# The value projection beside query and key, and V placed by DMA through DRAM

## The chip, the cores and the metric

The kernel runs on one core of a Trainium2 chip. The metric is the device time of one execution in microseconds (us); smaller is better. One execution was also taken by the hardware profiler, and its trace is what is read here.

## What is computed

Eight batches of 256 tokens with 128 features go through one transformer layer. Attention has 16 heads of 8 dimensions, and a token sees only tokens at most 32 away. A mixture of 8 experts follows.

```
h    = layernorm(x) * (1 + ca) + sa
qkv  = h @ W_qkv.T                      # Q, K, V: 16 heads of 8
attn = softmax(Q K^T / sqrt(8) within 32 tokens)
x    = x + ga * (attn V) @ W_o.T
h    = layernorm(x) * (1 + cb) + sb
x    = x + gb * experts(h)              # top 2 of 8, silu(g) * u @ down
```

## The kernel before

One engine program is written by hand for each engine, and semaphores tie them together. The work is a software pipeline over the eight batches. In step `i` every engine does the attention of batch `i`, the part after attention (output projection, second norm, routing) of batch `i - 1`, the experts of batch `i - 2`, and the query and key projection of batch `i + 1`. The order inside a step is the order of the calls in each engine's `step`, and an engine executes its program strictly in that order. TensorE is PE, VectorE is DVE, ScalarE is ACT, GpSimd is POOL, SyncE is SP.

A batch is cut in 8 key blocks of 32 tokens (`NKB`, `KB`). The 16 heads are 4 groups (`NHG`) of 4 (`G`), and in `v_bd` the four heads `g` of a group have 32 partitions each. The names that matter below:

- `h_t` (128 features x 256 tokens) is written by ACT in `modulate_x` (L387). `project_qk` (L531 key, L532 query) and `project_v` (L539) read it on PE. In `step` on PE `project_v(i)` stands after `scores(i, 0)` and `transpose_o(i - 1)`, and `project_qk(i + 1)` stands after `down`.
- `keep_k` (DVE, L805) and `keep_q` (ACT, L393) copy the projections from PSUM (the bank groups `W2` and `W0`) to `k_bd` and `q_sb`, which `scores` needs.
- `keep_v` (ACT, L402) copies V from PSUM bank `OB` into `v_bd`, the block-diagonal operand that holds, for each key block and group of heads, 32 columns of V and 4 columns that sum the denominator. Each of its 16 copies takes 32 partitions x 64 elements. It stands between the exponentials of half 0 and `tanh_gate(i - 2, 1)`.
- `weigh_values` (PE, L583) multiplies `v_bd` with the probabilities. Its first call in a step, for half `t = 0`, waits for `v_ready` of that batch.
- `scores(i, t)` (L552, and L559 for the mask) is followed by `block_max` (DVE, L813), `row_maximum` (L831), `subtract_max` (PE, L567) and `exponentials` (ACT, L435). `activate` (DVE, L905 and L909) gates the experts, `weigh_experts` (POOL, L323) scales them, `transpose_act` (PE, L636) and `down` (L643) finish them.
- `route_input` (ACT, L417) hands the logits (PE, L594) to the routing chain on DVE, which ends in `cw` (L897).
- SP's queue carries the loads of `x` (L266) and the stores of `out` (L270). A store waits for `out_ready`.

## Time and profile before

| | before |
|---|---|
| median of 3 runs | 197.63 us (197.5 to 197.66) |
| the profiled execution's own time | 195.44 us |
| its span in the trace | 193.7 us |
| PE busy | 151.8 us, 78% |
| DVE busy | 141.0 us, 73% |
| ACT busy | 99.9 us, 52% |
| POOL busy | 49.6 us, 26% |

The span is the time between the first and the last instruction in the trace; the execution's own time holds 1.7 us more around it. Busy shares are means over stages with different limits, so no engine that is at 78% need be the limit at a given moment. The trace lists instructions in order of time. An engine's idle time stands in square brackets with the engine, tile and line that ended it.

### The profile page before, as it was taken

What the parts mean: (1) busy time and instruction counts of PE and PEld (TensorE: products, weight loads), DVE (VectorE), ACT (ScalarE), POOL (GpSimd) and SP (SyncE); (2) the same over time, 40 slices, a digit from 0 to 9 for tenths busy, and PEclk for the clock granted to TensorE, in tenths of its full rate; (3) what the DMA queues carried; (4) which work ended last, traced back from release to release, by engine and by line L of the source; (5) the groups of instructions that cost most, each with busy time, mean ns of one, the idle gap of its engine ahead of it and who ended that gap; (6) DMA issues with size and microseconds to landing.
All of it is one profiled execution on the core that took longest, in us unless ns stands there. A gap on an engine that the chain in (4) does not pass through costs nothing.

```text
span 193.7 us, 5025 instructions
## 1 busy us (share of the span) xinstructions
PE 151.8 (78%) x1948; PEld 126.1 (65%) x1948; DVE 141.0 (73%) x381; ACT 99.9 (52%) x262; POOL 49.6 (26%) x79
## 2 busy tenths in 40 slices
PE   1653986869995998699877987799779976975944
PEld 1553966658774885588656866596558765954744
DVE  2477166466779798788969796979697959856762
ACT  3170543945385538663667457654944494543420
POOL 5070000112052123232233205320530143224130
PEclk9995899975999999999999999999999999999987
DMA  5910000100000020001000010000000000000001
GB/s 141 279 41 0 3 3 0 30 3 0 3 0 0 3 54 3 0 5 36 21 3 3 8 50 0 2 3 27 3 0 3 27 5 0 5 27 0 0 0 54
DMA packets 5831, 4.12 MB, mean 21 GB/s; under 512 B 816, under 2 KB 5424, under 8 KB 5808
## 3 DMA queue, kind: packets, MB, share of 16 engines
q1 hardware_dynamic: 5664, 3.80, 6.9%
q8 instruction: 15, 0.25, 0.5%
q14 instruction: 8, 0.07, 0.1%
q10 hardware_dynamic: 144, 0.00, 0.0%
HBM read 2.76 MB, written 1.05 MB: 20 GB/s over the span
## 4 chain that ended last, share of the span: by engine, by line
PE 48%; DVE 23%; issue 19%; POOL 4%; ACT 4%; DMA 1%; DVEq 0%; POOLq 0%; ACTq 0%
PE ps L552 9%; DVE blkmax L813 8%; PE ps L643 7%; PE ps L583 7%; PE ps L567 4%; DVE gate_a L905 3%; POOL act_w L323 3%; PE ps L621 3%; DVE act L909 3%; DVE xn L790 3%; PE ps L636 3%; PE ps L623 2%; PE ps L622 2%; PE ps L594 2%; PE ps L531 2%
## 5 line engine op out<-in xcount | busy, mean ns | idle before, releaser
L813 DVE TRANSPOSE_TENSOR_REDUCE blkmax<-ps 128x44 f32<-128x1408 f32 x16 | 26.4, 1647 | 17.1 <-PE ps L559 17.1
L323 POOL TENSOR_TENSOR act_w<-act,cw 128x512 f32<-128x512 f32 x15 | 15.6, 1043 | 67.8 <-issue 48.7
L583 PE MATMUL ps<-probs,v_bd 128*36 128x64 f32 (+2 forms) x640 | 23.6, 229 | 8.4 <-ACT v_bd L402 8.4
L583 PEld LDWEIGHTS ps<-probs,v_bd 128*36 128x36 f32 x640 | 21.6, 115 | 12.8 <-issue 12.3
L402 ACT ACTIVATE v_bd<-ps 32x64 f32<-32x64 f32 x128 | 27.4, 214 | 1.8 <-PE ps L539 0.4
L435 ACT ACTIVATE probs<-ps 128x704 f32<-128x704 f32 x32 | 23.0, 756 | 5.2 <-PE ps L567 5.0
L552 PEld LDWEIGHTS ps<-q_sb,k_bd 32*128 32x128 f32 x640 | 19.3, 186 | 3.4 <-issue 2.4
L552 PE MATMUL ps<-q_sb,k_bd 32*128 32x96 f32 (+2 forms) x640 | 21.3, 274 | 0.1
L636 PE MATMUL ps<-con,act_w 128*128 128x128 f32 x64 | 10.3, 283 | 11.4 <-POOL act_w L323 5.7
L448 ACT ACTIVATE tanh_g<-ps 128x512 f32<-128x512 f32 x16 | 9.6, 597 | 17.6 <-PE ps L623 16.6
L567 PE MATMUL ps<-shift,quad_ones 128*128 128x384 f32 x64 | 16.7, 386 | 1.6 <-DVE shift L831 0.8
L643 PE MATMUL ps<-wd_sb,act_t 128*128 128x128 f32 x128 | 17.4, 293 | 0.7 <-ACT act_t L452 0.7
L643 PEld LDWEIGHTS ps<-wd_sb,act_t 128*128 128x128 f32 x128 | 16.5, 207 | 1.0 <-ACT act_t L452 0.9
L636 PEld LDWEIGHTS ps<-con,act_w 128*128 128x128 f32 x64 | 6.8, 142 | 14.7 <-POOL act_w L323 7.5
L805 DVE TENSOR_TENSOR k_bd<-ps,con 128x1024 f32<-128x1024 f32 x8 | 9.8, 1226 | 8.1 <-DVE ebeat L853 4.7
L452 ACT ACTIVATE act_t<-ps 128x512 f32<-128x512 f32 x16 | 9.6, 598 | 11.6 <-PE ps L636 11.6
L831 DVE TENSOR_TENSOR shift<-row_max,con 128x256 fp32r<-128x256 f32 x32 | 15.1, 513 | 0.6
L621 PE MATMUL ps<-w_hi,h_hi 128*128 128x512 f32 x32 | 14.0, 437 | 1.6 <-DVE act L909 1.4
L442 ACT ACTIVATE o_t<-ps 36x512 f32<-36x512 f32 x16 | 9.5, 592 | 9.3 <-PE ps L583 9.1
L567 PEld LDWEIGHTS ps<-shift,quad_ones 128*128 128x128 f32 x64 | 11.0, 206 | 4.0 <-DVE shift L831 3.3
L341 POOL TENSOR_TENSOR out_sb<-y_g,x 128x256 f32<-128x256 f32 x7 | 5.1, 726 | 32.1 <-DVE y_g L937 32.1
L790 DVE TENSOR_SCALAR xn<-x_sb,mv,rstd 128x128 f32<-128x128 f32 x16 | 11.3, 748 | 2.2 <-POOL rstd L307 2.2
(96 smaller groups left out, 276.9 us busy)
## 6 DMA issues: line engine op xcount, KB each, us to landing
x_sb<-x SPq DMA_DIRECT2D x8, 128.0 KB, 2.4
out<-out_sb SPq DMA_DIRECT2D x7, 128.0 KB, 1.8
wgu_sb<-w_gu SPq DMA_DIRECT2D x1, 512.0 KB, 4.2
wm_sb<-wmod SPq DMA_DIRECT2D x1, 256.0 KB, 4.0
wd_sb<-w_down SPq DMA_DIRECT2D x1, 256.0 KB, 5.8
con<-consts SPq DMA_DIRECT2D x1, 244.0 KB, 3.5
wqkv_sb<-wqkv SPq DMA_DIRECT2D x1, 192.0 KB, 3.6
wm_sb<-wmod SPq DMA_DIRECT2D x1, 128.0 KB, 2.7
```

The lines of the kernel that those rows point to most:

```text
L323: nc.gpsimd.tensor_tensor(act_w[:, t, :].rearrange("p (e i) -> p e i", e=E), act[:, t, :].rearrange("p (e i) -> p e i", e=E), view(cw[:, t ...
L402: last = nc.scalar.activation(dst, src, ACT.Copy)
L435: nc.scalar.activation(probs[:, t, hgs, cols], ps[:, hgs, cols], ACT.Exp, scale=float(DH) ** -0.5).then_inc(probs_ready, 1)
L552: nc.tensor.matmul(view(ps[:, hg, at:at + 1], [[(QBT - 1) * KB, hi - lo + 1], [1, KB]]), k_bd[rows, kb].rearrange("p g k -> p (g k)"), vie ...
L567: last = nc.tensor.matmul(ps[:, hg, 0:CELLS * KB], quad_ones[:], view(shift[:, hg, 0:1], [[0, 3], [1, QBT * KB]]), start=False, stop=True, ...
L583: last = nc.tensor.matmul(ps[p0:p0 + VW, OB, c0 + lo * KB:c0 + (hi + 1) * KB], v_bd[:, kb, hg, :], view(probs[:, t, hg, at:at + 1], [[-(QB ...
L621: nc.tensor.matmul(ps[:, bank, :], h2_hi[:, tok], w_hi[:, w], start=True, stop=False)
L636: last = nc.tensor.transpose(ps[:, W0 + t, c * 128:(c + 1) * 128], act_w[:, t, c * 128:(c + 1) * 128], ident)
L643: last = nc.tensor.matmul(ps[:, down_bank(b, t), t * D:(t + 1) * D], act_t[:, t, c, :], wd_sb[:, c, :], start=(c == 0), stop=(c == NC_ - 1))
L790: nc.vector.tensor_scalar(xn[:, t, :], xs[:, t, :], mv[:, t, 0:1], rs[:, t:t + 1], ALU.subtract, ALU.mult).then_inc(ready, 1)
L813: nc.vector.tensor_reduce(blkmax[:, t, :, live(t):live(t) + LIVE], view(ps[:, 0, live(t) * KB:live(t) * KB + 1], [[BANK, NHG], [KB, LIVE], ...
L831: nc.vector.tensor_tensor(shift[:, pair * PAIR:(pair + 1) * PAIR].rearrange("p h (q k) -> p (h q) k", k=KB), view(row_max[:, pair * PAIR, ...
```

## The change

PE's `project_qkv` now computes key, query and value for batch `i + 1` in one place, and V goes to the upper half of bank `W0`. ACT copies V once, 128 x 256, into `v_sb`. SP then stores `v_sb` in a DRAM buffer `v_spill`, waits for that, and issues four loads that put 8-element (32-byte) pieces on the diagonal of `v_bd`, which now has two buffers. The columns of `h_t` are written in the order (row in block, block), so that what one partition of `v_bd` takes from one head `g` is contiguous in DRAM; `keep_q` and `keep_k` undo that order when they read PSUM, and the V columns of the weight are reordered on the host.

```diff
 VW = G * DH + G
+VB = 2
+BY_ROW = [[1, NKB], [NKB, KB]]
...
         k_bd = sb("k_bd", [128, NKB, G, KB])
-        v_bd = sb("v_bd", [128, NKB, NHG, VW])
+        v_sb = sb("v_sb", [128, G, NT, NHG * DH])
+        v_bd = sb("v_bd", [128, VB, NKB, NHG, VW])
...
         def down_bank(b, t):
...
             return {B - 2: OB, B - 1: 2 + t}.get(b, W1)
-        def value_block(source, g):
-            dst = v_bd[g * KB:(g + 1) * KB, source:source + 1, 0:1, g * DH:g * DH + 1]
-            src = ps[source * KB:(source + 1) * KB, OB, g * DH:g * DH + 1]
-            return (view(dst, [[NSRC * NHG * VW, NT], [VW, NHG], [1, DH]]),
-                    view(src, [[D, NT], [G * DH, NHG], [1, DH]]))
...
+            def place_values(b):
+                wait(sp, v_kept, b, 1, 1)
+                sp.dma_start(v_spill[b % VB].rearrange("g (t p) d -> p (g t) d", p=128),
+                             v_sb[:].rearrange("p g t d -> p (g t) d")).then_inc(v_spilled, 16)
+                wait(sp, v_spilled, b, 16, 16)
+                wait(sp, pv_ps, b - VB, PARTS, PARTS)
+                for g in range(G):
+                    sp.dma_start(v_bd[g * KB:(g + 1) * KB, b % VB, :, :, g * DH:(g + 1) * DH]
+                                 .rearrange("p k h d -> p (k h) d"),
+                                 v_spill[b % VB, g].rearrange("(r k) (h d) -> r (k h) d", k=NKB, h=NHG))\
+                      .then_inc(v_ready, 16)
             def step(i, pre, tail, ffn):
...
                     load_x(i + 2)
+                if pre:
+                    place_values(i + 1)
...
                 sp.dma_start(dst[:], src).then_inc(w_loaded, 16)
+            sp.wait_ge(dens_made, 1)
+            place_values(0)
...
             def modulate_x(b):
...
                 wait(act_e, xt_ps, b, 1, 1)
-                wait(act_e, v_ps, b, 1, 0)
-                nc.scalar.activation(h_t[:], ps[:, W0, 0:S], ACT.Identity, scale=mod[:, CA, b:b + 1],
+                wait(act_e, qv_ps, b, 1, 0)
+                nc.scalar.activation(view(h_t[:, 0:1], BY_ROW), ps[:, W0, 0:S], ACT.Identity, scale=mod[:, CA, b:b + 1],
...
             def keep_q(b):
-                wait(act_e, q_ps, b, 1, 1)
+                wait(act_e, qv_ps, b, 1, 1)
                 wait(act_e, scores_ps, b, QT * NHG, 0)
-                nc.scalar.activation(q_sb[:], ps[:, W0, 0:S], ACT.Copy).then_inc(q_ready, 1)
+                nc.scalar.activation(q_sb[:], view(ps[:, W0, 0:1], BY_ROW), ACT.Copy).then_inc(q_ready, 1)
...
             def keep_v(b):
...
-                wait(act_e, v_ps, b, 1, 1)
-                wait(act_e, pv_ps, b, PARTS, 0)
-                for source in range(NSRC):
-                    for g in range(G):
-                        dst, src = value_block(source, g)
-                        last = nc.scalar.activation(dst, src, ACT.Copy)
-                last.then_inc(v_ready, 1)
+                wait(act_e, qv_ps, b, 1, 1)
+                wait(act_e, v_spilled, b, 16, 0)
+                nc.scalar.activation(v_sb[:], view(ps[:, W0, S:S + 1], [[NHG * DH, G], [D, NT], [1, NHG * DH]]), ACT.Copy)\
+                  .then_inc(v_kept, 1)
...
             def modulate_h2(i):
...
                     keep_gates(2 * i + 1)
-                if i > 0:
-                    keep_v(i)
...
                     keep_q(i + 1)
+                    keep_v(i + 1)
...
             def transpose_x(b):
                 wait(pe, actt_ready, b - 3, NT, 1)
+                wait(pe, v_kept, b, 1, 0)
...
-            def project_qk(b):
+            def project_qkv(b):
...
                 nc.tensor.matmul(ps[:, W2, 0:S], wqkv_sb[:, 1], h_t[:], start=True, stop=True).then_inc(k_ps, 1)
-                nc.tensor.matmul(ps[:, W0, 0:S], wqkv_sb[:, 0], h_t[:], start=True, stop=True).then_inc(q_ps, 1)
-            def project_v(b):
-                wait(pe, h_ready, b, 1, 1)
-                wait(pe, o_ready, b - 1, 2, 2)
+                nc.tensor.matmul(ps[:, W0, 0:S], wqkv_sb[:, 0], h_t[:], start=True, stop=True)
                 for t in range(NT):
-                    last = nc.tensor.matmul(ps[:, OB, t * D:(t + 1) * D], h_t[:, t * 128:(t + 1) * 128],
+                    last = nc.tensor.matmul(ps[:, W0, S + t * D:S + (t + 1) * D], h_t[:, t * 128:(t + 1) * 128],
                                             wqkv_sb[:, 2], start=True, stop=True)
-                last.then_inc(v_ps, 1)
+                last.then_inc(qv_ps, 1)
...
             def scores(i, t):
...
             def weigh_values(i, t, pair):
...
                 if t == 0 and pair == 0:
-                    wait(pe, v_ready, i, 1, 1)
+                    wait(pe, v_ready, i, G * 16, G * 16)
+                    wait(pe, o_ready, i - 1, 2, 2)
...
                         at = cell(t, kb, lo) * KB
-                        last = nc.tensor.matmul(ps[p0:p0 + VW, OB, c0 + lo * KB:c0 + (hi + 1) * KB], v_bd[:, kb, hg, :],
+                        last = nc.tensor.matmul(ps[p0:p0 + VW, OB, c0 + lo * KB:c0 + (hi + 1) * KB], v_bd[:, i % VB, kb, hg, :],
...
                     if b + 2 < B:
-                        wait(pe, q_ready, b + 2, 1, 1)
+                        wait(pe, v_kept, b + 2, 1, 1)
...
                     transpose_o(i - 1)
-                if i > 0:
-                    project_v(i)
...
                 if pre:
-                    project_qk(i + 1)
+                    project_qkv(i + 1)
...
             pe.wait_ge(qkv_loaded, 16)
-            project_qk(0)
-            project_v(0)
+            project_qkv(0)
...
                 wait(dve, scores_ps, b, QT * NHG, 0)
-                nc.vector.tensor_tensor(k_bd[:], view(ps[:, W2, 0:1], [[KB, NKB], [0, G], [1, KB]]),
+                nc.vector.tensor_tensor(k_bd[:], view(ps[:, W2, 0:1], [[1, NKB], [0, G], [NKB, KB]]),
...
             dve.wait_ge(zeroed, 3)
-            nc.vector.tensor_copy(view(v_bd[:, 0, 0, G * DH:G * DH + 1], [[VW, NKB * NHG], [1, G]]),
-                                  view(con[:, C_DEN:C_DEN + 1], [[0, NKB * NHG], [1, G]])).then_inc(dens_made, 1)
+            nc.vector.tensor_copy(view(v_bd[:, 0, 0, 0, G * DH:G * DH + 1], [[VW, VB * NKB * NHG], [1, G]]),
+                                  view(con[:, C_DEN:C_DEN + 1], [[0, VB * NKB * NHG], [1, G]])).then_inc(dens_made, 1)
...
         "x": t(a["L0_attn_x"]),
-        "wqkv": t(wqkv.reshape(3, D, D).transpose(2, 0, 1)),
+        "wqkv": t(np.stack([wqkv[0:D].T, wqkv[D:2 * D].T,
+                            wqkv[2 * D:].T.reshape(D, NHG, G, DH).transpose(0, 2, 1, 3).reshape(D, D)], axis=1)),
...
     out = nc.dram_tensor("out", (B, S, D), F32, kind="ExternalOutput").ap()
-    program(nc, out=out, **aps)
+    v_spill = nc.dram_tensor("v_spill", (VB, G, S, NHG * DH), F32, kind="Internal").ap()
+    program(nc, out=out, v_spill=v_spill, **aps)
```

On PE, the end of step 2 and the start of step 3 (`L531` key, `L532` query, `L583` values, `L552` scores, `L559` mask, `L656` transpose of `o_t`, `L539` V, `L621` experts up); before:

```order
L531 MATMUL ps<-h_t,wqkv_sb 128x256 [waits ex_ready,h_ready]
L532 MATMUL ps<-h_t,wqkv_sb 128x256
L583 MATMUL ps<-probs,v_bd 36x32 [waits probs_ready]
...
L552 MATMUL ps<-q_sb,k_bd 128x2x32 [waits probs_ready,q_ready,k_ready]
...
L559 MATMUL ps<-mask_bf,rep_bf 128x2x128 x4
L656 MATMUL ps<-con,o_t 128x100 [waits k_ready,ex_ready,o_ready]
L656 MATMUL ps<-con,o_t 128x100 x3
L539 MATMUL ps<-wqkv_sb,h_t 128x128 [waits o_ready,h_ready]
L539 MATMUL ps<-wqkv_sb,h_t 128x128
L621 MATMUL ps<-w_hi,h_hi 128x512 [waits h2_lo_ready,yg_ready,h2_hi_ready,q_ready]
```

and with the change (`L540`, `L541` and `L543` are key, query and V, `L588` values, `L556` scores, `L563` mask, `L661` transpose, `L626` experts up):

```order
L540 MATMUL ps<-h_t,wqkv_sb 128x256 [waits ex_ready,h_ready]
L541 MATMUL ps<-h_t,wqkv_sb 128x256
L543 MATMUL ps<-wqkv_sb,h_t 128x128 x2
L588 MATMUL ps<-probs,v_bd 36x32 [waits probs_ready]
...
L556 MATMUL ps<-q_sb,k_bd 128x2x32 [waits probs_ready,q_ready,k_ready]
...
L563 MATMUL ps<-mask_bf,rep_bf 128x2x128 x4
L661 MATMUL ps<-con,o_t 128x100 [waits k_ready,ex_ready,o_ready]
L661 MATMUL ps<-con,o_t 128x100 x3
L626 MATMUL ps<-w_hi,h_hi 128x512 [waits h2_lo_ready,yg_ready,h2_hi_ready,v_kept]
```

The two V matmuls moved from behind the transposes of `o_t` to a place ahead of `weigh_values(i, 1, ...)` and `scores(i + 1, 0)`.

On ACT, step 3 of before (`L435` exponentials, `L402` copies of V, `L448` tanh, `L409` and `L412` the second modulation, `L452` and `L417` experts and routing):

```order
L435 ACTIVATE probs<-ps 128x2x352 [waits pv_ps,shifted_ps] x2
L402 ACTIVATE v_bd<-ps 32x2x4x8 [waits pv_ps,v_ps]
L402 ACTIVATE v_bd<-ps 32x2x4x8 x15
L448 ACTIVATE tanh_g<-ps 128x512 [waits gate_a_ready,up_ps]
L409 ACTIVATE h_t<-ps,mod 128x256 [waits up_ps,h2t_ps]
L412 ACTIVATE h_hi<-h_t 128x256 [waits h2_ready]
L452 ACTIVATE act_t<-ps 128x512 [waits actt_ps] x2
L417 ACTIVATE ex<-ps 128x16 [waits route_step,logits_ps]
```

and with the change, from the end of step 2 into step 3 (`L405` and `L411` are the copies of q and V, `L451` the copy of `o_t`, `L444` exponentials, `L457` tanh):

```order
L399 ACTIVATE h_t<-ps,mod 128x8x32 [waits qv_ps,xt_ps]
L444 ACTIVATE probs<-ps 128x2x352 [waits pv_ps,shifted_ps]
L405 ACTIVATE q_sb<-ps 128x256 [waits scores_ps,qv_ps]
L411 ACTIVATE v_sb<-ps 128x256 [waits v_spilled,qv_ps]
L451 ACTIVATE o_t<-ps 36x512 [waits ot_ps,pv_ps]
L451 ACTIVATE o_t<-ps 36x512
L457 ACTIVATE tanh_g<-ps 128x512 [waits gate_a_ready,up_ps]
L436 ACTIVATE on_t<-ps 128x256 [waits ont_ps]
L444 ACTIVATE probs<-ps 128x2x352 [waits pv_ps,shifted_ps] x2
L457 ACTIVATE tanh_g<-ps 128x512 [waits gate_a_ready,up_ps]
```

The sixteen copies between exponentials and tanh are gone. One copy stands behind that of q, and ahead of that of `o_t`.

On SP's queue, before, from the first store on:

```order
L270 DMA out<-out_sb 128x2x128 [waits out_ready]
L266 DMA x_sb<-x 128x2x128 [waits x1_ready]
L270 DMA out<-out_sb 128x2x128 [waits out_ready]
L266 DMA x_sb<-x 128x2x128 [waits x1_ready]
L270 DMA out<-out_sb 128x2x128 [waits out_ready]
```

and with the change:

```order
L271 DMA v_spill<-v_sb 128x8x32 [waits v_kept]
L276 DMA v_bd<-v_spill 32x32x8 [waits pv_ps,v_spilled]
L276 DMA v_bd<-v_spill 32x32x8 x3
L265 DMA out<-out_sb 128x2x128 [waits out_ready]
L261 DMA x_sb<-x 128x2x128 [waits x1_ready]
L271 DMA v_spill<-v_sb 128x8x32 [waits v_kept]
L276 DMA v_bd<-v_spill 32x32x8 [waits pv_ps,v_spilled]
L276 DMA v_bd<-v_spill 32x32x8 x3
```

Between a load of `x` and the next store now stand one DMA to DRAM and four DMAs of 32 x 32 x 8 elements, with a wait between them.

## Rows read from the trace of the kernel before

**Rows 1.** Page, part 5: costliest groups of instructions, two of its lines.

```profile
L583 PE MATMUL ps<-probs,v_bd 128*36 128x64 f32 (+2 forms) x640 | 23.6, 229 | 8.4 <-ACT v_bd L402 8.4
...
L402 ACT ACTIVATE v_bd<-ps 32x64 f32<-32x64 f32 x128 | 27.4, 214 | 1.8 <-PE ps L539 0.4
```

**Rows 2.** Waits by engine and line: total us, times, longest us.

```profile
PE ps L583 <- ACT v_bd L402: 8.4, 7, 2.4
```

**Rows 3.** Timeline, middle of step 4: start us, us, engine, line, operation [idle before].

```profile
98.74 1.65 DVE L813 TRANSPOSE_TENSOR_REDUCE blkmax<-ps 128x44 f32<-128x1408 f32 x1 [1.44 <-PE ps L559]
...
99.61 1.44 PE L583 MATMUL ps<-probs,v_bd 128*36 128x64 f32 x40 [0.99 <-ACT v_bd L402]
...
100.79 0.69 DVE L905 SCALAR_TENSOR_TENSOR gate_a<-tanh_g,ps 128x512 f32<-128x512 f32 x1
...
102.33 1.04 POOL L323 TENSOR_TENSOR act_w<-act,cw 128x512 f32<-128x512 f32 x1 [3.60 <-issue]
```

**Rows 4.** Chain that ended last, step 4: start us, us, engine, line.

```profile
90.93 1.65 DVE blkmax L813
...
103.43 0.66 PE ps L636 x4
...
107.37 0.43 PE ps L531 x2
...
109.61 1.25 PE ps L552 x40
111.09 1.65 DVE blkmax L813
```

**Rows 5.** Timeline, first and last microseconds of step 4.

```profile
91.16 0.63 PE L539 MATMUL ps<-wqkv_sb,h_t 128*128 128x128 f32 x4
...
93.34 0.44 PE L663 MATMUL ps<-con,o_n 128*128 128x128 f32 x2 [0.15 <-DVE o_n L918]
...
108.27 0.38 ACT L393 ACTIVATE q_sb<-ps 128x256 f32<-128x256 f32 x1 [1.36 <-PE ps L532]
...
110.68 0.29 PE L559 MATMUL ps<-mask_bf,rep_bf 32*128 32x256 bf16 x4
...
110.94 0.17 DVE L897 TENSOR_TENSOR cw<-wsel,rsum 128x16 f32<-128x16 f32 x1
```

**Rows 6.** Timeline, steps 0 to 2: the first wait for `v_bd`.

```profile
30.38 1.65 DVE L813 TRANSPOSE_TENSOR_REDUCE blkmax<-ps 128x44 f32<-128x1408 f32 x1 [2.02 <-PE ps L559]
...
39.79 0.56 DVE L790 TENSOR_SCALAR xn<-x,mv,rstd 128x128 f32<-128x128 f32 x2
...
40.24 1.97 PE L583 MATMUL ps<-probs,v_bd 128*36 128x64 f32 x40 [2.44 <-ACT v_bd L402]
...
42.86 0.56 ACT L409 ACTIVATE h_t<-ps,mod 128x256 f32<-128x256 f32 x1 [2.77 <-PE ps L519]
...
43.57 0.99 PE L594 MATMUL ps<-gw_sb,h_t 128*128 128x8 f32 x4 [0.32 <-ACT h_t L409]
...
47.11 1.22 DVE L805 TENSOR_TENSOR k_bd<-ps,con 128x1024 f32<-128x1024 f32 x1
...
50.63 1.65 DVE L813 TRANSPOSE_TENSOR_REDUCE blkmax<-ps 128x44 f32<-128x1408 f32 x1 [0.98 <-PE ps L559]
```

**Rows 7.** Windows: length, busy us (and count) per engine, PE clock, DMA share, GB/s.

```profile
41.00:42.00 1.00, 1.00 (x23) 1.00 (x17) 0.76 (x2) 0.00 (x0) 0.00 (x0) 0.50 0.06 16
```

**Rows 8.** DMA queue q10 from 0.7 to 2.7 us: packets, MB, share of 16 engines.

```profile
q10 hardware_dynamic: 144, 0.00, 3.7%
```

**Rows 9.** DMA queue q1 from 130.2 to 132.2 us, one store alone, same columns.

```profile
q1 hardware_dynamic: 272, 0.13, 22.9%
```

**Rows 10.** Page, part 6: DMA issues, KB each, median us from issue to landing.

```profile
x_sb<-x SPq DMA_DIRECT2D x8, 128.0 KB, 2.4
out<-out_sb SPq DMA_DIRECT2D x7, 128.0 KB, 1.8
```

**Rows 11.** Tile `x_sb` on SP's queue: time of one issue, ns min/median/max.

```profile
L266 SPq DMA_DIRECT2D x_sb<-x x8: 368/453/476, 0.7 to 110.7; - x8
```

More of the change, by code:

```diff
@@ L109, in view, with program @@
     return bass.AP(ap.tensor, ap.offset, [list(ap.ap[0])] + [list(d) for d in dims])
-def program(nc, x, wqkv, wo, gate_w, bias, w_gu, w_down, c_t, wmod, consts, out):
+def program(nc, x, wqkv, wo, gate_w, bias, w_gu, w_down, c_t, wmod, consts, v_spill, out):
     with ExitStack() as ctx:
@@ L203, in program @@
         out_stored, last_ready, last_actw_ready = sem("out_stored"), sem("last_ready"), sem("last_actw_ready")
-        xt_ps, k_ps, q_ps, v_ps = sem("xt_ps"), sem("k_ps"), sem("q_ps"), sem("v_ps")
+        xt_ps, k_ps, qv_ps = sem("xt_ps"), sem("k_ps"), sem("qv_ps")
         scores_ps, shifted_ps, pv_ps = sem("scores_ps"), sem("shifted_ps"), sem("pv_ps")
@@ L219, in program @@
             sem("h_ready"), sem("q_ready"), sem("k_ready"), sem("probs_ready"), sem("o_ready"), sem("ont_ready"))
-        v_ready, h2_hi_ready = sem("v_ready"), sem("h2_hi_ready")
+        v_kept, v_spilled, v_ready, h2_hi_ready = sem("v_kept"), sem("v_spilled"), sem("v_ready"), sem("h2_hi_ready")
         h2_ready, ex_ready, tanh_ready, actt_ready = (
```

## The prediction

> **What bounds the kernel now.** I read the costliest groups first, then the waits, then the timeline of one step of the steady part, and last the chain that ended last, because the edit takes work from ACT, which is busy only 52% of the span. The groups show what the change aims at: 128 copies of V cost ACT 27.4 us, and before `weigh_values` PE idled 8.4 us for them [rows 1]. The waits put this in seven pieces, of which the longest is 2.4 us [rows 2]. So one piece is special, and the other six are about 1 us each.
>
> The timeline of step 4 (from one first `block_max` at 90.93 to the next at 111.09, a period of 20.16 us [rows 4]) shows whether such a piece counts. The mask of the second scores releases DVE at 98.74. PE then waits 0.99 us and starts `weigh_values` at 99.61. But DVE goes on without a wait: `block_max`, then `gate_a` at 100.79 (no idle time stands in its row, so it did not wait for ACT's tanh), then the second `act`, and POOL's `act_w` from 102.33 to 103.37 [rows 3]. The chain takes that road: PE's transposes L636 start at 103.43, released by POOL [rows 4]. PE's 1.44 us of `weigh_values` would end at 100.2 instead of 101.1 and PE would wait longer for the same POOL result. In the steady part ACT's copies are worth nothing.
>
> From 103.43 on PE has no gap: L531 at 107.37, `scores` at 109.61, mask until 110.97 (110.68 + 0.29), and `block_max` starts 0.12 us later, at 111.09 [rows 4, 5]. DVE's routing chain ends at 111.11 (110.94 + 0.17) [rows 5], that is, at the same moment. PE is the bound of the last part of a step, with DVE level beside it.
>
> Step 1 is different. There PE waits 2.44 us for `v_bd` until 40.24, and runs `weigh_values` until 42.21, though DVE's `xn` was done at 40.35 (39.79 + 0.56). ACT's `h_t` starts only at 42.86, and the routing follows [rows 6]. After this wait PE's clock is 0.50, the 1.2 GHz level [rows 7], and the logits L594 take 0.99 us [rows 6].
>
> **The change, part by part. V's matmuls.** Their count stays. They leave a place where PE waits for DVE in any case: after the experts' first half PE still waited 0.15 us for `o_n` before L663 [rows 5], and that wait grows to about 0.6 us. So nothing is saved there. They arrive between L531/L532 and `weigh_values`, in the part where PE has no gap. Price: the two fp32 matmuls of L531 with 256 columns take 0.43 us on the chain [rows 4]; V has four of 128 columns, the same sum. Their own row says 0.63 us with the pipeline's fill [rows 5]. I take 0.43 and keep 0.63 as the upper bound; 0.3 is the lower one, should 0.12 us of hand-over overlap. The first `block_max` of step 1 also waited for PE (2.02 us of idle before 30.38 [rows 6]), so that step pays too.
>
> **Copies on ACT.** Sixteen copies of 0.214 us [rows 1] become one of the size of q's, 0.38 us [rows 5], at a place where ACT otherwise waits for PE. q's copy now comes after V's matmuls: 108.23 + 0.43, copied by 109.1, V by 109.5. `scores` can't start before 109.61 + 0.43, so both are covered by about 0.5 us. The strided views of `h_t`, q and k move the same 256 or 1024 elements. `k_bd` takes 1.22 us for 1024 elements [rows 6], already over one nanosecond each; I add nothing. If its strided read cost more, the first 0.43 us would be free, because DVE now has that much room before `block_max`.
>
> **Start.** `v_bd` doubles, so its clearing on POOL and the denominators on DVE do too, before the first projection; I take 0. The first q is 0.8 us later behind V, which the wait of DVE after start covers.
>
> **Step 1.** With V placed in time, the transposes can start at 40.35 instead of 42.21, 1.86 us earlier. At full clock the logits take half of 0.99, which gives 0.5 more. The routing on DVE and then `k_bd` come 2.35 us earlier, at 44.76 instead of 47.11; `k_bd` ends at 45.98, scores and mask take 1.48 (111.09 - 109.61), and `block_max` starts at 47.46 instead of 50.63: 3.17 us. PE itself would win more (1.86, and about 2 of the 5 us that it runs at the half clock), less 0.43 for V, so DVE's road decides and V's matmuls of this step are hidden. Less the 0.43 of step 0's end: 2.74 us gained.
>
> **Placing by DMA.** Each batch needs one DMA out and four in. A DMA has 1024 pieces and 16 for the semaphore, 65 for each of 16 engines; all five 325. The trace has no such DMA, so I bound the time X of a piece. Small pieces of 32 bytes: 144 packets took 3.7% of 16 engines in 2.0 us, 8.2 ns each [rows 8]. Pieces of 512 bytes: 272 took 22.9% of the same time, 26.9 ns each [rows 9]. A store lands after 1.8 us [rows 10], 0.46 of them its own 17 packets per engine, which leaves 1.34; a load after 2.4, which leaves 1.94. An issue takes SP at most 0.48 us [rows 11]. V is copied at 109.5. At 8.2 ns the store lands at 109.5 + 1.34 + 0.53 = 111.4, the last load at 111.4 + 3 x 0.48 + 1.94 + 0.53 = 115.3. `weigh_values` could use it first at 98.6 + 20.16 + 0.43 = 119.2, and needs it only when PE's slack is used up, at 99.61 + 0.9 + 20.59 = 121.1. At 26.9 ns the last load lands at 121.5, 0.4 us late. The break-even is (121.1 - 112.8)/0.325 = 25.5 ns. I take the lower end, because the 32-byte row is the nearest in kind, and cost the placement at 0. The store of `out` now stands behind this on SP's queue; nobody waits for it but `out_sb`'s next use a step later. The next load of `x` comes after it, 4 us later than now, and is used a step later.
>
> The Trainium skill speaks against this part: its page "DMA: Bandwidth & Descriptors" (section Specifications) asks for at least 512 bytes per piece, and says that below this the engine reads, modifies and writes. If each piece so costs at least what a 512-byte one does, the sum would be the one at 26.9 ns. The 32-byte loads of this trace do not show it (8.2 ns); no row shows a small piece written to DRAM.
>
> **The sum.** -2.74 + 5 x 0.43 (the first `block_max` of steps 3 to 7) = -0.6, with -3.2 for the gain of step 1 at best and 0.63 for V at worst the other way. I round to -0.5. The profiled execution took 195.44 us for a span of 193.7; this gives 194.9. The runs' median is 197.63, 2.2 above it, and I carry the difference over: 197.1 us. A measurement of this kernel can tell about 0.2%, 0.4 us, from no change.
>
> **Rivals.**
> - *Small pieces are slow (slower).* One mechanism: a piece of 32 or 128 bytes takes over 25.5 ns in sustained flow, `v_ready` comes late, and PE waits at `weigh_values` in each step. For it: 4096 pieces in a row were never seen here. Against: 8.2 ns. At 35 ns it is 3.1 us late in each of six steps and step 1 gains nothing: 197.6 + 18.6 + 3.0 = 219 us. 15%.
> - *The clock stays low in step 1 (slower).* PE is then idle from about 39.7 to 40.8 only, and the 0.99 us gaps of later steps never cost the clock; but if it falls, step 1 gains 1.86 - 0.43 - 0.86 = 0.6, and the total is +1.6: 199.2 us. 10%.
> - *V's matmuls are hidden (faster).* If DVE, level with PE at 111.1, sets the end of the step, they cost nothing: -3.2, 194.5 us. Against: the mask's end to `block_max` is 0.12 us, a plain hand-over. 12%.
> - *The whole wait comes off (faster).* ACT's removed 0.99 us per step counts after all: 8.4 less, 3.0 for V, 192.2 us. Against: PE's next wait is for DVE and POOL. 5%.
> - *The forecast*, 58%: 195.9 to 198.6 us, from V at 0.3 to 0.63 us in five steps and step 1 between 3.2 and 2.2 of gain. Of this 28 are below -0.4 us, 20 within, 10 above.
>
> Faster 28 + 12 + 5 = 45%, the same 20%, slower 10 + 15 + 10 = 35%. The range takes in the hidden V on one side and the low clock on the other, with 0.8 above it: 194.5 to 200.0.
>
> **What the profile would show.** PE's wait for `v_bd` is gone in all seven places and the next wait of PE, for DVE `act`, is longer by 0.9 us. The period of a step is 20.6 us and DVE waits for PE's mask before each first `block_max`. Step 1 keeps the full clock and ends near 48. The last load of `v_bd` lands 6 us after ACT's copy, well before `weigh_values`. What would make the forecast wrong: a wait of L588 for a DMA, a period still at 20.16, or the clock at half speed after 41 us.

## The result, and the profile after

The changed kernel takes 206.57 us (median of four executions, 203.99 to 207.47) where the kernel before took 197.56 in the same call: a ratio of 1.049 [1.043, 1.056], slower by 9 us. I had forecast 197.1 us. The profiled execution took 207.47 us for a span of 205.7, against 195.44 and 193.7. Here and below, medians and ranges are of all executions, but a ratio is formed from the quicker ones alone where a kernel's times fall in two groups, which matters most for no_dma and no_dma_again (the others lie up to 12 us above) and for old_place_filled (three of ten at 198.0 to 199.6 us).

From the page of the kernel after, part 1 (busy time of TensorE, its share of the span, instructions), part 2 (TensorE's granted clock in tenths, in 40 slices) and part 3 (the hardware queue):

```profile
PE 164.5 (80%) x1948; PEld 139.4 (68%) x1948; DVE 141.0 (69%) x381; ACT 77.9 (38%) x142; POOL 50.5 (25%) x79
...
PEclk9999999966996699958998899999999999996797
...
q1 hardware_dynamic: 47264, 5.90, 18.4%
```

And from the page of the kernel before, the same clock line:

```profile
PEclk9995899975999999999999999999999999999987
```

TensorE executes 1948 matmuls as before, but is busy 12.7 us longer (151.8 before). The clock line shows where: between a fifth and three fifths of the span, where the kernel before has one dip and then nothing but 9, the kernel after has dip upon dip.

The waits of TensorE in the kernel after (us in total, times, longest):

```profile
PE ps L527 <- DVE xn L792: 8.2, 9, 1.3
PE ps L668 <- DVE o_n L920: 5.6, 7, 2.0
PE ps L641 <- POOL act_w L335: 5.5, 8, 2.3
PE ps L641 <- DVE act L911: 5.5, 6, 0.9
```

The wait for `v_bd` [rows 2] is gone from the list, and no wait for a DMA has taken its place: `weigh_values` (now L588) starts without idle time. Most of its 8.4 us has moved to the next wait on TensorE's row: L527 waits 8.2 us for DVE's `xn`, where the same transposes waited 1.5 us before. L668 waits 0.60 us a step for `o_n`, where L663 waited 0.15 [rows 5], as forecast.

What this does is seen in the timeline of TensorE in the kernel after, middle of step 3 (start us, us, engine, line, operation, count, idle before):

```profile
82.50 0.29 PE L563 MATMUL ps<-mask_bf,rep_bf 32*128 32x256 bf16 x4
82.72 1.44 PE L588 MATMUL ps<-probs,v_bd 128*36 128x64 f32 x40
85.19 0.41 PE L527 MATMUL ps<-con,xn 128*128 128x128 f32 x2 [1.03 <-DVE xn L792]
86.50 0.63 PE L641 MATMUL ps<-con,act_w 128*128 128x128 f32 x4 [0.91 <-DVE act L911]
87.59 1.12 PE L641 MATMUL ps<-con,act_w 128*128 128x128 f32 x4 [0.46 <-POOL act_w L335]
88.50 0.86 PE L599 MATMUL ps<-gw_sb,h_t 128*128 128x8 f32 x4
89.21 1.63 PE L571 MATMUL ps<-shift,quad_ones 128*128 128x384 f32 x4
```

The same rows of the kernel before (step 4), of which [rows 3] showed the third:

```profile
98.33 0.29 PE L559 MATMUL ps<-mask_bf,rep_bf 32*128 32x256 bf16 x4
...
101.02 0.41 PE L519 MATMUL ps<-con,xn 128*128 128x128 f32 x2
102.34 0.63 PE L636 MATMUL ps<-con,act_w 128*128 128x128 f32 x4 [0.91 <-DVE act L909]
103.43 0.66 PE L636 MATMUL ps<-con,act_w 128*128 128x128 f32 x4 [0.46 <-POOL act_w L323]
```

Before, the idle time was 0.99, then 1.44 us of `weigh_values`, then 0.91 and 0.46. After, it is 1.03, 0.91 and 0.46 with only 1.0 us of work between them. Over 5 us the amount is the same, 2.60 us busy after and 2.64 before. In the 3.2 us that end where the second group of transposes (L641, L636) starts, it is not: 1.04 us after and 1.86 before. In the windows, the columns are length, busy us and count by engine, granted clock, DMA share, GB/s. After:

```profile
82.60:87.60 5.00, 2.60 (x55) 1.96 (x47) 4.66 (x8) 1.41 (x3) 1.42 (x3) 0.98 0.02 5
84.20:87.40 3.20, 1.04 (x6) 0.62 (x6) 3.17 (x7) 1.21 (x3) 0.91 (x1) 1.00 0.01 3
```

Before:

```profile
98.60:103.60 5.00, 2.64 (x51) 2.15 (x49) 4.80 (x8) 3.00 (x8) 1.40 (x3) 1.00 0.01 2
100.20:103.40 3.20, 1.86 (x36) 1.35 (x30) 3.17 (x8) 1.38 (x3) 1.07 (x2) 1.00 0.00 0
```

At the end of the joined idle, in the slice from 87 us on, the clock goes to 0.50, the 1.2 GHz level, and stays there until 94. The second L641 then takes 1.12 us instead of 0.66 [rows 4], and on the chain of step 3 the down projection L648 takes 3.26 us, where the same line takes 1.79 in step 5 at full clock. Four steps of the kernel after in windows (same columns), each from one first `block_max` to the next:

```profile
75.11:98.69 23.58, 20.21 (x240) 17.35 (x240) 16.96 (x46) 9.35 (x17) 5.74 (x9) 0.86 0.17 23
98.69:120.75 22.06, 18.68 (x240) 15.83 (x240) 16.96 (x45) 9.34 (x17) 5.75 (x9) 0.92 0.19 26
120.75:141.35 20.60, 17.20 (x240) 14.32 (x240) 16.97 (x46) 9.12 (x17) 5.73 (x9) 1.00 0.21 27
141.35:161.93 20.58, 17.21 (x240) 14.32 (x240) 16.95 (x45) 9.12 (x17) 5.74 (x9) 1.00 0.18 21
```

The same 240 matmuls and the same DVE time, but 3 us more where the clock is 0.86. At full clock the period is 20.6 us, as I had forecast.

**Where the 12.0 us of span come from**, by the first `block_max` of each step: 1.40 up to step 1 (31.78 against 30.38), -0.24 in step 1, 3.16 in step 2, 3.44 in step 3, 1.90 in step 4, 0.47 and 0.45 in steps 5 and 6, 1.42 from the last one to the end (43.77 against 42.35). In that last part TensorE has two half-clock stretches (186 to 193 and 200 to 203 us), where the kernel before has one (188 to 191 us).

### The profile page after: what moved, and what is told of

Read it like the earlier page. It is cut to its first block, busy times and chain, and to the rows that moved or that the text cites. A ratio compares the mean times of both kernels' runs of the same rounds, so it can differ in the third digit from the quotient of the medians.

```text
span 205.7 us, 4947 instructions
## 1 busy us (share of the span) xinstructions
PE 164.5 (80%) x1948; PEld 139.4 (68%) x1948; DVE 141.0 (69%) x381; ACT 77.9 (38%) x142; POOL 50.5 (25%) x79
## 3 DMA queue, kind: packets, MB, share of 16 engines
q1 hardware_dynamic: 47264, 5.90, 18.4%
## 4 chain that ended last, share of the span: by engine, by line
PE 52%; DVE 24%; issue 17%; POOL 4%; DMA 1%; ACT 1%; DVEq 0%; POOLq 0%
PE ps L556 8%; PE ps L648 8%; DVE blkmax L815 8%; PE ps L588 6%; PE ps L571 6%; PE ps L641 3%; DVE gate_a L907 3%; POOL act_w L335 3%; DVE act L911 3%; PE ps L626 3%; PE ps L696 3%; DVE xn L792 3%; PE ps L599 2%; PE ps L628 2%; PE ps L627 2%
## 5 line engine op out<-in xcount | busy, mean ns | idle before, releaser
L444 ACT ACTIVATE probs<-ps 128x704 f32<-128x704 f32 x32 | 23.2, 762 | 6.2 <-PE ps L571 6.0
L588 PE MATMUL ps<-probs,v_bd 128*36 128x64 f32 (+2 forms) x640 | 23.9, 232 | 0.0
L588 PEld LDWEIGHTS ps<-probs,v_bd 128*36 128x36 f32 x640 | 21.8, 117 | 2.3 <-issue 1.5
L556 PEld LDWEIGHTS ps<-q_sb,k_bd 32*128 32x128 f32 x640 | 20.3, 195 | 4.0 <-issue 3.2
L556 PE MATMUL ps<-q_sb,k_bd 32*128 32x96 f32 (+2 forms) x640 | 22.3, 282 | 0.6 <-ACT q_sb L405 0.6
L648 PE MATMUL ps<-wd_sb,act_t 128*128 128x128 f32 x128 | 20.7, 329 | 0.7 <-ACT act_t L461 0.7
L641 PE MATMUL ps<-con,act_w 128*128 128x128 f32 x64 | 12.2, 323 | 11.2 <-POOL act_w L335 5.5
L648 PEld LDWEIGHTS ps<-wd_sb,act_t 128*128 128x128 f32 x128 | 20.1, 244 | 1.0 <-ACT act_t L461 0.9
L571 PE MATMUL ps<-shift,quad_ones 128*128 128x384 f32 x64 | 18.8, 424 | 1.6 <-DVE shift L833 0.8
L807 DVE TENSOR_TENSOR k_bd<-ps,con 128x1024 f32<-128x1024 f32 x8 | 9.8, 1225 | 13.7 <-issue 8.2
L457 ACT ACTIVATE tanh_g<-ps 128x512 f32<-128x512 f32 x16 | 9.5, 597 | 23.1 <-PE ps L628 22.2
L641 PEld LDWEIGHTS ps<-con,act_w 128*128 128x128 f32 x64 | 8.0, 161 | 14.7 <-POOL act_w L335 7.5
L626 PE MATMUL ps<-w_hi,h_hi 128*128 128x512 f32 x32 | 14.5, 454 | 1.4 <-DVE act L911 1.4
L418 ACT ACTIVATE h_t<-ps,mod 128x256 f32<-128x256 f32 x8 | 4.5, 564 | 28.7 <-PE ps L527 28.7
L571 PEld LDWEIGHTS ps<-shift,quad_ones 128*128 128x128 f32 x64 | 12.8, 233 | 3.7 <-DVE shift L833 3.3
L527 PE MATMUL ps<-con,xn 128*128 128x128 f32 x32 | 7.7, 328 | 8.3 <-DVE xn L792 8.2
L627 PE MATMUL ps<-w_lo,h_hi 128*128 128x512 f32 x32 | 13.0, 406 | 0.0
```

Of the source, the lines that this page charges most:

```text
L444: nc.scalar.activation(probs[:, t, hgs, cols], ps[:, hgs, cols], ACT.Exp, scale=float(DH) ** -0.5).then_inc(probs_ready, 1)
L556: nc.tensor.matmul(view(ps[:, hg, at:at + 1], [[(QBT - 1) * KB, hi - lo + 1], [1, KB]]), k_bd[rows, kb].rearrange("p g k -> p (g k)"), vie ...
L571: last = nc.tensor.matmul(ps[:, hg, 0:CELLS * KB], quad_ones[:], view(shift[:, hg, 0:1], [[0, 3], [1, QBT * KB]]), start=False, stop=True, ...
L588: last = nc.tensor.matmul(ps[p0:p0 + VW, OB, c0 + lo * KB:c0 + (hi + 1) * KB], v_bd[:, i % VB, kb, hg, :], view(probs[:, t, hg, at:at + 1] ...
L626: nc.tensor.matmul(ps[:, bank, :], h2_hi[:, tok], w_hi[:, w], start=True, stop=False)
L627: nc.tensor.matmul(ps[:, bank, :], h2_hi[:, tok], w_lo[:, w], start=False, stop=False)
```

## The experiments

Twelve runs in three calls. The kernel before had medians of 195.49, 195.81 and 196.62 us in them, so each ratio is to the kernel before of its own call. Periods are read from the rows of `block_max`; "half clock" is the time at the 1.2 GHz level between the first `block_max` of step 2 and the end of step 6, summed from the granted clock in windows of 1 us. Steps and half clock are those of the one profiled execution.

| kernel | median us (range) | ratio | steps 1, 2, 3, 4 (us) | half clock us, steps 2 to 6 |
|---|---|---|---|---|
| before | 197.56 | | 20.25, 20.16, 20.14, 20.16 | 0 |
| after | 206.57 | 1.049 | 20.01, 23.32, 23.58, 22.06 | 17 |
| one_copy | 204.66 (203.29 to 205.89) | 1.049 [1.042, 1.057] | 17.99, 20.14, 20.13, 22.67 | 17 |
| v_moved | 200.39 (199.98 to 200.43) | 1.027 [1.024, 1.030] | 21.31, 20.60, 20.58, 20.58 | 3 |
| wait_back | 206.13 (205.09 to 208.63) | 1.055 [1.049, 1.061] | 17.65, 22.20, 23.44, 23.66 | 20 |
| filled | 197.31 (196.78 to 198.34) | 1.013 [1.007, 1.019] | 17.65, 22.19, 20.57, 20.59 | 3 |
| wait_back24 | 200.58 (199.28 to 202.03) | 1.024 [1.016, 1.032] | 18.74, 22.18, 20.58, 20.58 | 3 |
| no_dma | 203.69 (199.52 to 206.38) | 1.022 [1.011, 1.033] | 17.65, 22.20, 23.38, 23.62 | 20 |
| old_place_filled | 194.99 (194.01 to 199.59) | 0.995 [0.991, 0.999] | 18.23, 20.14, 20.14, 20.15 | 0 |
| before_filled1 | 197.03 (196.19 to 198.49) | 1.006 [1.002, 1.010] | 20.40, 20.31, 20.30, 20.30 | 0 |
| after_again | 205.82 (199.42 to 207.98) | (none given) | 17.66, 22.21, 23.52, 23.68 | 20 |
| no_dma_again | 204.53 (199.50 to 211.83) | 1.020 [1.014, 1.027] | 17.66, 22.19, 23.37, 23.63 | 20 |
| old_place | 194.97 (193.74 to 196.47) | 0.997 [0.994, 1.001] | 17.66, 21.72, 20.12, 20.26 | 7 |
| one_copy_filled | 193.65 (191.55 to 194.41) | 0.987 [0.981, 0.994] | 17.23, 20.15, 20.15, 20.15 | 3 |

The last column parts the kernels. Where the idle of TensorE is joined (after, after_again, one_copy, wait_back, no_dma, no_dma_again) it is 17 to 20 us; where the idle is divided by a wait or filled with work it is 0 to 7 us. It is not always 0: four such kernels keep one stretch of 3.4 us each (filled and wait_back24 in step 2, v_moved and one_copy_filled in step 6), and old_place two (steps 2 and 4).

**one_copy: the sixteen copies, and with them the wait, taken out of the kernel before.**

```diff
-                for source in range(NSRC):
-                    for g in range(G):
-                        dst, src = value_block(source, g)
-                        last = nc.scalar.activation(dst, src, ACT.Copy)
-                last.then_inc(v_ready, 1)
+                nc.scalar.activation(v_sb[:], ps[:, OB, 0:NT * D], ACT.Copy).then_inc(v_ready, 1)
```

> The kernel before, but ACT copies V once (128 x 256, to a tile that nobody reads) instead of sixteen times; v_bd is not filled, so this leaves the placing of V out. V's matmuls stay in their old place, no DMA is added. Theory A (the removed wait at weigh_values joins PE's idle stretches and the clock falls inside steps): half-clock stretches in two or three of the steps 2 to 6, 198 to 203 us. Theory B (the clock falls because V's matmuls left the place ahead of L663 and opened a hole of 0.6 us there): no fall, step 1 gains about 2.7 us, 195 us. Theory C (the DMAs of small pieces disturb PE): no fall, 195 us.

Measured: 204.66 us, above the range of every theory, in the direction of the first. It has less work on ACT than the kernel before, no DMA, and V's matmuls at their old place, and is slower by 4.9%. Its timeline of TensorE in step 4 has the joined idle of the kernel after, and behind it a clock that falls (L633's eight matmuls in 2.20 us):

```profile
99.23 0.41 PE L516 MATMUL ps<-con,xn 128*128 128x128 f32 x2 [1.03 <-DVE xn L787]
100.54 2.20 PE L633 MATMUL ps<-con,act_w 128*128 128x128 f32 x8 [0.91 <-DVE act L906]
```

Taking the copies and their wait away is enough to make the kernel slower.

**v_moved: V's matmuls moved, sixteen copies and their wait kept.** Not in the cut: V is lifted once to `v_sb`, and the sixteen copies read it there and not in PSUM.

```diff
+                for t in range(NT):
+                    last = nc.tensor.matmul(ps[:, W0, S + t * D:S + (t + 1) * D], h_t[:, t * 128:(t + 1) * 128],
+                                            wqkv_sb[:, 2], start=True, stop=True)
+                last.then_inc(qv_ps, 1)
...
-                if i > 0:
-                    project_v(i)
```

> The kernel before, with V's matmuls moved beside query and key and lifted once to SBUF, but the sixteen copies into v_bd kept at their old place on ACT, so the wait of PE at weigh_values stays. No DMA. Theory A (removed wait): the clock as in before, 7 x 0.43 us more for V, 200.6 us. Theory B (hole ahead of L663): half-clock stretches inside steps, 203 us or more. Theory C (DMAs): 200.6 us.

Measured: 200.39 us, with periods of 20.6 us in steps 2 to 5 and a half-clock stretch of 6.8 us in step 1, as before. The price of V's place is read there: 0.44 us a step. Of the number itself some is luck. It was worked out from a kernel before of 197.6 us, and the one of this call took 195.49; the kernel is slower by 4.9 us, not 3.0. Step 0 (16.49 us for 15.42), step 1 (21.31 for 20.25) and step 6 (20.83 for 20.13, with a half-clock stretch from 145 us on) hold the rest. Nor was the wait kept at its size: the sixteen copies take 4.21 us instead of 3.61, and the wait is 1.56 us. The copies of the kernel before, then two rows of v_moved, step 4 of each:

```profile
95.86 3.61 ACT L402 ACTIVATE v_bd<-ps 32x64 f32<-32x64 f32 x16
```

```profile
98.94 4.21 ACT L406 ACTIVATE v_bd<-v_sb 32x64 f32<-32x64 f32 x16
103.25 1.44 PE L587 MATMUL ps<-probs,v_bd 128*36 128x64 f32 x40 [1.56 <-issue]
```

**wait_back and wait_back24: the wait returned to the kernel after, by useless copies.**

```diff
+                    wait(act_e, q_ready, i, 1, 1)
+                    for n in range(16):
+                        last = nc.scalar.activation(spare[:, n, :], q_sb[0:32, 0:64], ACT.Copy)
+                    last.then_inc(held, 1)
...
+                    wait(pe, held, i, 1, 0)
```

> The changed kernel, with sixteen small copies of no use put back on ACT in the old place, and weigh_values waits for the last of them: only the wait is put back. Theory A: clock as in before, 197.6 + 3.0 for V = 200.6 us, faster than the changed kernel by 5 although it does more. Theories B and C: 206 us or more, unchanged.

Measured: 206.13 us, which missed the theory's number. The row of ScalarE shows that the edit had not done what it was for: these sixteen copies took 2.43 us instead of 3.61, so the last one ended at 102.11 us, before the mask (102.13), and `weigh_values` did not wait in steps 2 to 6:

```profile
99.68 2.43 ACT L481 ACTIVATE spare<-q_sb 32x64 f32<-32x64 f32 x16
```

So it became a control: the same copies without the wait help nothing. With 24 of them (`range(24)`):

> The changed kernel with a wait of ScalarE put ahead of TensorE's first weighing of values: 24 useless copies of 32x64 from SBUF (0.152 us each by the run wait_back, 3.65 us together, against 3.43 us of the 16 removed ones) are queued at the place in ScalarE's row where the removed copies stood, and the weighing waits for the last one. In wait_back 16 such copies took 2.43 us and ended before the weighing was due. Theory A (the removed wait joined two idle stretches of TensorE and the clock falls there): with the wait returned, some 0.9 us of idle stands before the weighing again, the half-clock stretches after 50 us go, and the time is that of v_moved, 200 to 201 us where the changed kernel takes 205 to 207. Theory B (the placement's DMA or the issue on the sync queue disturbs something): it stays at 205 to 207 us.

Measured: 200.58 us, 6 us less than the kernel after by the medians (5 by the ratios, 1.024 for 1.049), by adding 24 copies and a wait. The half-clock stretch in step 2 stayed, against the expectation; those of steps 3 and 4 are gone. The timeline of wait_back24 in step 4 has the idle in two parts again:

```profile
102.29 1.44 PE L595 MATMUL ps<-probs,v_bd 128*36 128x64 f32 x40 [0.96 <-issue]
103.73 0.41 PE L533 MATMUL ps<-con,xn 128*128 128x128 f32 x2
105.05 0.63 PE L648 MATMUL ps<-con,act_w 128*128 128x128 f32 x4 [0.91 <-DVE act L918]
```

"Issue" stands there for the wait for the last copy. TensorE is no busier for it: 17.28 us in this step (window below), against 17.20 in a full-clock step of the kernel after. What differs is where the idle lies.

```profile
93.65:114.23 20.58, 17.28 (x240) 14.35 (x240) 16.97 (x46) 12.50 (x41) 5.75 (x9) 1.00 0.21 28
```

**filled: four useless matmuls in the idle of the kernel after.**

```diff
+            def fill(i, n):
+                wait(pe, x1_ready, i, 1, 1)
+                for _ in range(n):
+                    nc.tensor.matmul(ps[:, W2, S:S + D], ident, wqkv_sb[:, 2], start=True, stop=True)
...
                 weigh_values(i, 0, 1)
+                if tail:
+                    fill(i - 1, 4)
                 if tail:
                     transpose_x1(i - 1)
```

> The changed kernel, with four matmuls of no use (128 columns fp32, 0.22 us each) on PE between weigh_values of half 0 and the transposes of xn, where it idles 1.03 us. Theory A and B: the clock stays at 1.00 in the steps, 197 to 198 us, the time that was forecast. Theory C (DMAs, or anything but PE's idle time): 206 us or more.

Measured: 197.31 us. More work on TensorE, 9 us less time by the medians, 7 by the ratios (1.013 for 1.049). The fillers take 1.16 us where 1.03 us were idle, and the clock holds from step 3 to the end of step 6. In step 2 (22.19 us) it still fell at 62.1 us, though the gap was filled. Step 4:

```profile
100.81 1.16 PE L704 MATMUL ps<-wqkv_sb,con 128*128 128x128 f32 x8
101.91 0.41 PE L527 MATMUL ps<-con,xn 128*128 128x128 f32 x2
103.23 0.63 PE L641 MATMUL ps<-con,act_w 128*128 128x128 f32 x4 [0.91 <-DVE act L918]
```

**no_dma and no_dma_again: the placement left out.** The edit removes the store, the four loads and the waits for them.

```diff
                 wait(sp, v_kept, b, 1, 1)
-                sp.dma_start(v_spill[b % VB].rearrange("g (t p) d -> p (g t) d", p=128),
...
-                wait(act_e, v_spilled, b, 16, 0)
...
-                    wait(pe, v_ready, i, G * 16, G * 16)
```

> The changed kernel without any placement: v_sb is copied once, no DMA moves it, so the block-diagonal operand stays at its initial contents (this kernel leaves out the placing of V; everything else runs). Theory A (clock): 47264 small packets less change nothing, 204 to 207 us with half-clock stretches in steps 2 to 4 as in the changed kernel. Theory B (DMA traffic or the queue): the time falls to 196 to 199 us.

> The changed kernel without the placement's DMAs (the placing of V is left out), in more rounds: the first time it gave 203.69 us, between the two theories' numbers. Theory A (the clock): the same as after_again within 1%. Theory B (the DMAs share the blame): below after_again by 1.5% or more in the interval of the ratios.

> The changed kernel once more, to stand beside the three others of this call on one chip. Both theories: 204 to 207 us, with half-clock stretches in steps 2 to 4. [...]

Measured: 203.69, just under the first theory's range, then 204.53 beside 205.82 for the kernel after on the same chip, each with executions from 199.5 up to 208 or more. Their medians differ by 0.6%, less than either spreads; six executions of each, spread so widely, can't exclude some 2% (my estimate from their spread). The profiles say more: no_dma_again and after_again have the same step times within 0.2 us, at full clock (steps 1 and 6) within 0.01. Of the 47,264 packets 41,600 are gone and the slow steps are still there, so they are not what slows the kernel.

**old_place_filled, old_place: V's matmuls back, the single copy and the placement kept.**

```diff
+            def project_v(b):
+                wait(pe, h_ready, b, 1, 1)
+                wait(pe, o_ready, b - 1, 2, 2)
                 for t in range(NT):
-                    last = nc.tensor.matmul(ps[:, W0, S + t * D:S + (t + 1) * D], h_t[:, t * 128:(t + 1) * 128],
+                    last = nc.tensor.matmul(ps[:, OB, t * D:(t + 1) * D], h_t[:, t * 128:(t + 1) * 128],
                                             wqkv_sb[:, 2], start=True, stop=True)
-                last.then_inc(qv_ps, 1)
+                last.then_inc(v_ps, 1)
...
                 if tail:
                     transpose_o(i - 1)
+                if i > 0:
+                    project_v(i)
```

> The single copy and the placement by DMA are kept, V's matmuls go back to where they stood before the change (behind the transposes of o, in the attention bank), and four useless 128x128 fp32 matmuls stand in TensorE's row before transpose_x1, as in the run filled. Theory A: V's matmuls are free again (0.43 us a step less than in filled, seven steps) and the clock is kept by the fillers: 194 us in a call whose kernel before takes 195.5, unless the placement, which now starts in the same step, lands late: the copy ends near 2.5 us after the step's start, the last piece lands some 7.5 us behind it, and the weighing is due some 8 us after the step's start, so up to 1.5 us a step may be waited for on the DMA, which gives 194 to 204. Rival (V's place does not matter, only idle does): as filled, 197 us.

> Single copy and placement by DMA kept, V's matmuls where they stood before the change, no fillers: old_place_filled without its four useless matmuls. In old_place_filled the weighing of values waited 0.57 us for the last piece of v_bd, so that here a wait stands where the removed one stood, and the idle ahead of transpose_x1 is shorter by it. Theory A: if the 0.57 us wait keeps the two idle stretches apart, the period is 20.14 us and the time that of old_place_filled, 195 us; if it is too short to do that, the clock falls as in one_copy, 200 to 205 us. Rival (the DMA placement costs by itself): 200 us or more with periods over 20.14 us at full clock.

Measured: 194.99 and 194.97 us. Neither is clearly faster than the kernel before. The ratio of old_place_filled, 0.995 [0.991, 0.999], comes within 0.1% of no change, and its executions reach up to 199.59 us. Its gain is step 1 (18.23 us for 20.25), less the 1.1 us by which its step 0 is longer (16.51 for 15.42); steps 2 to 4 are at 20.14 again. In old_place a wait stands before `weigh_values` again, for the last load of `v_bd` (step 4, where the clock was low for a while; the profile puts it down to "issue"), and in the steady steps the clock fell only twice: for 3.4 us in step 2, which took 21.72 us, and for 3.4 us in step 4, from the end of this wait on, which took 20.26. A wait of 0.6 to 1.5 us in the old place thus gives most of the time back, not all of it:

```profile
99.27 2.58 PE L592 MATMUL ps<-probs,v_bd 128*36 128x64 f32 x40 [1.45 <-issue]
```

**before_filled1: the fillers alone, in the kernel before** (the same `fill`, four matmuls).

> The kernel before, untouched but for the same four useless 128x128 fp32 matmuls before transpose_x1. Theory A (the clock alone decides): the half-clock stretch of step 1 (20.25 us) goes, step 1 takes 17.6 us, all else is as before, 193 us where the kernel before takes 195.5; if the fillers cost their 0.45 us in each of six steps, 195.5. Rival (step 1's half clock came from the wait for v_bd and the fillers are behind it, so that they cannot help): 195.5 to 198 us with step 1 at 20.2 us.

Measured: 197.03 us, slower by 0.6%: a miss for the first theory, a hit for the rival. The first theory wanted step 1 at 17.6 us; it took 20.40, though the half clock there shrank from 6.8 to 3.4 us. The steady steps cost 0.15 us more each (20.30 for 20.14). What sets step 1 of the kernel before is, by its rows, the wait for `v_bd` itself, still 2.45 us:

```profile
40.83 1.44 PE L583 MATMUL ps<-probs,v_bd 128*36 128x64 f32 x40 [2.45 <-ACT v_bd L402]
```

**one_copy_filled: one_copy with the fillers.**

> one_copy (the kernel before, V copied once to a tile that nothing reads, so V's placing is left out) with the four useless matmuls before transpose_x1. It says what the removed copies and their wait are worth when the clock is held. The prediction's step (a) says nothing in a steady step (period 20.14 us) and some 2.6 us in step 1: 192 to 193 us in a call whose kernel before takes 195.5. Rival (the removed wait is worth its 0.99 us a step once the clock is held): periods of 19.2 us, 187 us. If the fillers do not hold the clock without V's matmuls beside q and k, 200 us or more.

Measured: 193.65 us, 11 us below one_copy by four more matmuls a step. With the clock held, the removed copies are worth nothing in a steady step (20.15 us) and 3.0 us in step 1 (17.23). Step 6 took 21.64 us, with a half-clock stretch from 142 us on, behind a gap that was filled.

## Why the prediction was wrong

The step that failed is the one under "What bounds the kernel now": "PE's 1.44 us of `weigh_values` would end at 100.2 instead of 101.1 and PE would wait longer for the same POOL result. In the steady part ACT's copies are worth nothing." Of the first sentence one half is what the chip did: `weigh_values` ends earlier. But TensorE then waits for DVE's `xn`, ahead of L527, and the waits for `act` (0.91 us) and `act_w` (0.46) keep their size; the forecast had put the 0.9 us on the wait for `act`. The second sentence took idle time of TensorE as free wherever it stands, so that the term for a steady step was 0 where the runs show up to 3 us. The wait of 0.99 us lay ahead of 1.44 us of work; without it, 1.03 us of idle lies behind that work and runs into the 0.91 and 0.46 us that were there already. One rival spoke of the clock, and dismissed it: "the 0.99 us gaps of later steps never cost the clock". That was read from the kernel before, in which these gaps were apart; the change is what joins them.

Shown by runs: taking the copies and their wait away gives the loss (one_copy, +4.9%), copies without the wait do not help (wait_back), copies with the wait take 6 us off (wait_back24), filling the idle with work takes 9 us off (filled) or 11 (one_copy_filled). The DMAs are not needed for the loss (one_copy, no_dma). In the profiled execution the price is 8.50 us in steps 2 to 4, of which V's matmuls are 1.3 and the clock 7.2. Of the clock's part the joined idle accounts for all but what step 2 still loses with the idle filled or divided (22.19 and 22.18 us for 20.6): 1.6 us are not shown to be its work.

The Trainium skill's page "TensorE: Matmul & The Clock Gate" (section "Part 1: The HAM clock gate") says that activity releases the throttle and that the moment at which it does differs from run to run. These traces agree in part. In steps 2 to 4 of the kernel after the clock falls (at 63.5, 87.4 and 111.3 us) within 0.8 us of the second L641, which ends the sparse stretch, and six executions of this kernel spread from 199.42 to 207.98 us; but in filled it also fell, at 62.1 us, with the gap filled. The page also calls the penalty "<1% of a typical kernel span", but that is for the ramp at the start of a kernel; here a clock that falls again in mid-kernel cost 3.7% (7.2 of 193.7 us).

Step by step:

- **V's matmuls, +0.43 us a step**: right. Periods at full clock are 20.60 and 20.58 us after 20.13; L543's four matmuls stand on the chain with 0.44 us. The rival that they are hidden is out.
- **Up to step 1, +0.43**: too small. It was 1.40: V 0.44, 0.22 of a later start (the first `block_max` at 15.18 instead of 14.96), and 0.74 in the first half of step 0. The last is not the change's: one_copy_filled, with V's matmuls in the old place and no DMA, takes 16.46 us for step 0, the kernel before 15.42. The rows show TensorE slower for longer. Its first eight matmuls with `gates` take 2.08 us (before: 2.07, at a granted clock of 0.50), the next eight 1.86 (before: 1.05, at full clock), in the kernel after and before:

```profile
20.88 1.86 PE L696 MATMUL ps<-con,gates 128*128 128x128 f32 x8
```

```profile
20.59 1.05 PE L691 MATMUL ps<-con,gates 128*128 128x128 f32 x8
```

The granted clock of the kernel after reads 1.00 in this stretch, which the durations contradict, so that it is not to be trusted before step 1.

- **Step 1, 3.17 of gain (2.74 less step 0's part)**: too large by 0.6. With the clock held the step is 17.65 us for 20.25, a gain of 2.60 (filled, no_dma, after_again). The half-clock stretch of this step in the kernel before lasts 6.8 us (41.0 to 47.8), not the 5 that I had read. The profiled execution of the kernel after had a half-clock stretch from 43 us on and gained only 0.24: the rival "the clock stays low in step 1" in its place, but not its size, since I let it stop there.
- **The copies on ACT, 0**: right for ACT's own time; what their wait did for TensorE is the step that failed. V is lifted in 0.38 us, and the strided read of `k_bd` takes 1225 ns as before (1226).
- **Placing by DMA, 0**: right. In the queue listing of the kernel after, issue to landing:

```profile
v_spill<-v_sb SPq DMA_DIRECT2D x8, 128.0 KB, 2.2
v_bd<-v_spill SPq DMA_DIRECT2D x32, 32.0 KB, 2.7
```

V is copied at 96.53 us, the last load is issued by 101.4 and lands near 104, 7.4 us after the copy where I had said 6, and before `weigh_values` at 106.30. The rival of slow pieces (219 us) is out. The 41,600 added packets took 9.4 ns each by the difference of the queue's two shares (18.4% of 205.7 us, 6.9% of 193.7), near the 8.2 that I took. One term was mis-sized: an issue of a load takes SyncE 0.67 us, not 0.48 (550/665/1260 ns):

```profile
L276 SPq DMA_DIRECT2D v_bd<-v_spill x32: 550/665/1260, 13.5 to 164.0; - x32
```

- **What counts as a change, 0.4 us**: too small. The three executions behind it lie within 0.16 us, but in the later calls those of the kernel before spread from 194.5 to 198.3 us. The loss of 9 us is clear of this; old_place_filled against the kernel before is not.

**What stays open.** Steps 5 and 6 of the kernel after have the same idle rows as step 3 and keep the full clock; one_copy keeps it in steps 2 and 3 and loses it in step 4. In four kernels it falls once without the joined idle. Why the same pattern is punished in one step and not in the next is not settled by these runs; joined idle makes falls frequent, and is neither enough nor needed for a single one. Nor is the least amount of filling that would do, and a version in which V's own matmuls fill the idle was not tried.

## What to carry to other kernels

Idle time of TensorE can be free on the critical path and still not free for its clock: before a wait is removed, look where that idle goes on TensorE's row, and whether it then runs into the next gap. If the clock line of the profile gets new dips while the count of matmuls stays, put useful (or even useless) work into the longest gap and see whether the time comes back. A wait that divides two gaps may be worth more than the work that it costs.
